# A selective state-space layer: eight passes run as one sequence of 128 states

## The reference

```
x = silu(conv(x) + conv_b);  x_dbl = x @ Wx.T      # dt (64), B (16), C (16)
dt = softplus(dt @ Wdt.T + bdt);  A = -exp(A_log)
dA = exp(dt * A);  dBx = dt * x * B                # per channel and state
h = dA_t * h + dBx_t;  y_t = sum over n of h * C_t
y = (y + x * D) * silu(z);  out = y @ W_out.T
```

## Time and profile before

| | us |
|---|---|
| median of 3 runs | 3912.1 (3908.99 to 3917.67) |
| the profiled execution | 3909.11 |
| its span, first to last instruction | 3907.3 |
| VectorE busy over the span | 2598.5 (67%) |
| PE matmul busy | 3486.0 (89%) |
| ACT busy | 2154.5 (55%) |
| POOL busy | 1405.9 (36%) |

### The profile page before, as it was taken

One profiled execution on the slowest core, in us unless ns is written; L12 is line 12 of the kernel. 1 busy time (PEld: TensorE's weight loads), 2 busy tenths in 40 slices (PEclk: granted clock), 3 DMA queues, 4 the chain that ended last, 5 costly groups with the idle time before them and its releaser, 6 DMA issues. The chain is left out here.

```text
span 3907.3 us, 135959 instructions
## 1 busy us (share of the span) xinstructions
PE 3486.0 (89%) x57850; PEld 2873.7 (74%) x57851; DVE 2598.5 (67%) x4426; ACT 2154.5 (55%) x3392; POOL 1405.9 (36%) x1363
## 2 busy tenths in 40 slices
PE   6999999999884499929999999999878888898878
PEld 4888888888674366617888888888357777788767
DVE  5777777777544122237777777776878888889964
ACT  2666666666542122205666666666467777777732
POOL 3333333333031300052333333332056666667700
PEclk8999999999896799968999999999889999999989
DMA  2001001100006110020010001000011111111100
GB/s 69 29 30 35 29 29 33 33 29 20 11 1 238 56 32 30 30 89 20 29 37 29 29 29 37 29 29 4 25 36 40 39 39 40 37 41 44 39 24 22
DMA packets 60394, 148.31 MB, mean 38 GB/s; under 512 B 8194, under 2 KB 28706, under 8 KB 59458
## 3 DMA queue, kind: packets, MB, share of 16 engines
q1 hardware_dynamic: 56770, 131.70, 10.3%
q0 software_dynamic: 3072, 8.39, 0.7%
HBM read 123.29 MB, written 16.78 MB: 36 GB/s over the span
## 5 line engine op out<-in xcount | busy, mean ns | idle before, releaser
L654 ACT ACTIVATE x_probs<-x_score_ps 128x1024 f32<-128x1024 f32 (+1 forms) x896 | 814.5, 961 | 672.5 <-PE x_score_ps L563 666.0
L714 DVE TENSOR_REDUCE x_maxes<-x_misc_ps 128x1 f32<-128x512 f32 (+1 forms) x1792 | 1022.7, 628 | 27.3 <-PE x_misc_ps L481 21.2
L1873 POOL TENSOR_TENSOR b_drive<-b_b_all,b_dtx 128x1024 f32<-128x1024 f32 x256 | 596.8, 2369 | 399.2 <-DVE b_dtx L1949 377.0
L678 POOL CAST x_kT_hi<-x_kT 128x512 fp32r<-128x512 f32 (+1 forms) x448 | 257.9, 576 | 1232.0 <-ACT x_kT L627 1116.5
L1904 DVE TENSOR_TENSOR_SCAN b_state<-b_decay_ps,b_drive 128x512 f32<-128x512 f32 x512 | 589.9, 1209 | 15.1 <-POOL b_drive L1873 12.4
L557 PE MATMUL x_score_ps<-x_qz,x_kT 32*128 32x128 f32 x13312 | 590.3, 277 | 0.3 <-DVE x_shift L724 0.2
L557 PEld LDWEIGHTS x_score_ps<-x_qz,x_kT 32*128 32x128 f32 x13312 | 501.5, 182 | 3.6 <-issue 1.5
L531 PE MATMUL x_misc_ps<-x_probs,x_v 128*32 128x64 f32 x26624 | 464.7, 221 | 0.0
L531 PEld LDWEIGHTS x_misc_ps<-x_probs,x_v 128*32 128x32 f32 x26624 | 392.4, 110 | 65.8 <-issue 23.3
L481 PE MATMUL x_misc_ps<-x_kT_hi,x_qz_hi 32*128 32x512 f32 (+1 forms) x2048 | 422.1, 406 | 6.0 <-POOL x_kT_hi L678 4.1
L1809 ACT ACTIVATE b_decay_ps<-b_dt,b_a_neg 128x504 f32<-128x504 f32 x512 | 347.9, 680 | 69.2 <-DVE b_state L1904 69.2
(11 more groups left out here) (284 smaller groups left out, 5839.4 us busy)
## 6 DMA issues: line engine op xcount, KB each, us to landing
x_raw<-in_ctxT SPq DMA_DIRECT2D x64, 800.5 KB, 4.5
b_b_all<-b_b_rows SPq DMA_DIRECT2D x128, 256.0 KB, 3.3
m_w<-in_m_w SPq DMA_DIRECT2D x16, 704.0 KB, 19.3
m_w<-in_m_w SPq DMA_DIRECT2D x8, 768.0 KB, 20.2
m_slot_rows<-m_zero SPq DMA_DIRECT2D x1, 4992.0 KB, 17.0
m_block_rows<-m_slot_rows SPq DMA_DIRECT2D x39, 128.0 KB, 2.0
m_slot_out<-m_out SPq DMA_DIRECT2D x39, 128.0 KB, 1.7
x<-in_x SPq DMA_DIRECT2D x1, 2048.0 KB, 8.3
```

What stands on the lines that cost most here:

```text
L654: nc.scalar.activation(probs[rows, s % 2, js, 0:n], score_ps[rows, js, 0:n], ACT.Exp).then_inc(exp_done, 1)
L714: nc.vector.tensor_reduce(maxes[:, c:c + m, j, k0 // NB], bank(op)[:, 0:m * even].rearrange("p (c k) -> p c k", c=m)[:, :, 0:kn], AX.X, AL ...
L1873: nc.gpsimd.tensor_tensor(drive[:, k % 2, c:c + 2, :], b_all[:, k % 2:k % 2 + 1, :].broadcast_to([P, 2, NB]), dtx[:, c:c + 2, :], ALU.mult ...
```

## The change

`recur` no longer works pass by pass. There is one loop over 128 states, and all that stood between passes is put into slots inside them.

- The raw steps of a pass, its softplus and the product `dtx` are made during the pass before. `dt` has two buffers; the steps of the first two passes are made at the start, with their softplus.
- Softplus is written another way: c = min(v, 80), and (v - c) + ln(1 + exp(c)). At the start VectorE does min, subtract and add. For passes 2 to 7 POOL does them on two chunks at a time (`cap`, `excess`, `join`). ACT does `exponential` (one in each of states 8 to 11) and `logarithm` (all four in state 12). For pass 2, whose scratch `xc` of block 0 is free only when the outputs of pass 0 are made, they stand in states 13 to 15 of pass 1.
- PE does one extra piece a state, `besides`, between two gathers: a chunk of the skip term in states 0, 13, 14, 15 (straight into the accumulator), a step chunk in states 1 to 4, an output of 128 tokens by 128 features in states 5 to 12 (in pass 1 steps 1, 2, 11, 12 and outputs 3 to 10). Steps and outputs take a turn in the two banks of `turn_ps`, by the list `USES`. ACT copies a step out (Identity with the bias), VectorE adds an output to x.
- The gates of a pass are done after the second scan of state 1 of the next pass, the products of the next pass after the second scan of state 15. The first gather of a pass (`start=True`) waits for the gates.
- `drive` is a ring of three halves instead of four. The table `wx` moves into `project`, `a_neg` takes the place of `a_log`, and the dummy activation for the table load is gone.

Core of the diff:

```diff
+    def extra(k):
+        p, n = divmod(k, NS)
+        if n == 0 or n >= NS - 3:
+            return ("skip", 0 if n == 0 else n - (NS - 4))
+        if p == 0:
+            return None
+        steps, outs = ((1, 2, 11, 12), 3) if p == 1 else ((1, 2, 3, 4), 5)
+        if n in steps:
+            return ("step", p + 1, steps.index(n)) if p + 1 < PASSES else None
+        if outs <= n < outs + 2 * TPB:
+            return ("out", p - 1) + divmod(n - outs, 2)
+        return None
+    def softplus_at(p):
+        return ((13, 14), (13, 14), (14, 14, 14, 14), 14, (15, 15)) if p == 1 else ((5, 6), (7, 8), (8, 9, 10, 11), 12, (14, 14))
+    USES = [("rows", d) for d in range(2)]
+    for k in range(STATES):
+        USES += [("tile", k, i) for i in TURNED]
+        if extra(k) is not None and extra(k)[0] != "skip":
+            USES.append(extra(k))
...
     # tensor
+        for k in range(STATES):
+            pe.wait_ge(state_done, (k + 1) * CI)
+            turn(k, 1)
+            turn(k, 0)
+            if k > 0:
+                gather(k - 1, 2)
+            if k > 0 and k % NS == 0:
+                add_total(k // NS - 1)
+            turn(k, 3)
+            turn(k, 2)
+            gather(k, 0)
+            besides(k)
+            gather(k, 1)
     # scalar
+        for k in range(STATES):
+            if k > 0:
+                read_tile(k - 1, 0)
+            make_decay(k, 2)
+            if k > 0:
+                read_tile(k - 1, 1)
+            make_decay(k, 3)
+            if k > 0:
+                read_tile(k - 1, 2)
+            if k + 1 < STATES:
+                make_decay(k + 1, 0)
+            besides(k)            # step copy of k-1; Exp, or four Ln, of pass p+1
+            if k + 1 < STATES:
+                make_decay(k + 1, 1)
     # gpsimd
+            if h >= 3:
+                pool.wait_ge(state_done, (h - 2) * 2)
+            nc.gpsimd.tensor_tensor(drive[:, h % 3, :, :], ...)
+            for half in range(2):
+                make_drive(k, half)
+            if p > 0 and p + 1 < PASSES:
+                caps, excesses, _, _, joins = softplus_at(p)
+                for half in range(2):
+                    if caps[half] == n:
+                        cap(p + 1, half)
+                    if excesses[half] == n:
+                        excess(p + 1, half)
+                    if joins[half] == n:
+                        join(p + 1, half)
     # vector
+            scan(k, 0)
+            if k > 0:
+                sum_tile(k - 1)
+            scan(k, 1)
+            if n == 1 and p > 0:
+                gate(p - 1)
+            if n == NS - 1 and p + 1 < PASSES:
+                make_dtx(p + 1)
+            scan(k, 2)
+            scan(k, 3)
+            if k > 0 and extra(k - 1) is not None and extra(k - 1)[0] == "out":
+                add_output(extra(k - 1))
```

More of the change, by code:

```diff
@@ new lines, in recur @@
+    READS = {"act": 0, "dve": 0}
+    READ_AT = {}
+    for use in USES:
+        by = "dve" if use[0] == "out" or use[0] == "tile" and use[2] == SUMMED else "act"
+        READS[by] += 1
+        READ_AT[use] = (by, READS[by])
+    SUMS = []
+    for k in range(STATES):
+        if k > 0:
+            SUMS.append(("read", k - 1, 2))
+        if k > 0 and k % NS == 0:
+            SUMS.append(("total", k // NS - 1))
+        SUMS += [("read", k, 0), ("read", k, 1)]
+    SUMS += [("read", STATES - 1, 2), ("total", PASSES - 1)]
@@ new lines, in besides @@
+        def besides(k):
+            use = extra(k)
+            p = k // NS
+            if use is None:
+                return
+            if use[0] == "skip":
+                c = use[1]
+                nc.tensor.matmul(acc_ps[:, c, :], diag[:, direction(p)[0], c, :], xc[:, direction(p)[0], c, tokens(p)],
+                                 start=False, stop=True, skip_group_check=True)
+            elif use[0] == "step":
+                step(use[1], use[2], open_bank(use)).then_inc(turn_done, 1)
+            else:
+                output(use)
@@ L1801, in _, with make_decay @@
+        gather(STATES - 1, 2)
+        add_total(PASSES - 1)
+        for i in range(TPB):
+            for h in range(2):
+                output(("out", PASSES - 1, i, h))
     @block.scalar
     def _(act):
-        def make_decay(p, n, c):
-            q = (p * NS + n) * CI + c
+        def make_decay(k, c):
+            p, n = divmod(k, NS)
+            q = k * CI + c
             if n == 0:
                 act.wait_ge(dt_done, p * CI + c + 1)
+            if n == 0 and direction(p)[1] == 0 and c < 2:
+                act.wait_ge(edge_done, direction(p)[0] * 2 + c + 1)
@@ L1817, in read_tile @@
             if k > 0:
[L1818 to L1827 removed]
+                act.wait_ge(acc_done, SUM_AT["read", k - 1, r])
@@ new lines, in besides @@
+        def besides(k):
+            use = extra(k - 1) if k > 0 else None
+            if use is not None and use[0] == "step":
+                made(act, use)
+                keep_step(use[1], use[2], bank(use)).then_inc(act_free, 1)
+            p, n = divmod(k, NS)
+            if p > 0 and p + 1 < PASSES:
+                _, _, exps, logs, _ = softplus_at(p)
+                for c in range(CI):
+                    if exps[c] == n:
+                        exponential(p + 1, c)
+                if logs == n:
+                    for c in range(CI):
+                        logarithm(p + 1, c)
@@ L1967, in feed_forward @@
+        sum_tile(STATES - 1)
+        gate(PASSES - 1)
+        for i in range(TPB):
+            for h in range(2):
+                add_output(("out", PASSES - 1, i, h))
 def feed_forward(nc, x_sb, ident, a):
```

388 lines of the change are left out of this document (194 added, 194 removed).

## The result

| us | before | after |
|---|---|---|
| median of the runs | 3912.8 (3906.3 to 3917.7, 6 runs) | 3939.9 (3931.3 to 3947.7, 6 runs) |
| profiled execution | 3909.1 | 3941.8 |
| start of the recurrence to its first scan | 21.2 | 32.7 |
| first scan to the end of the last | 825.9 | 835.4 |
| last scan to the end of the last output addition | 17.0 | 19.5 |

The ratio of after to before is 1.0071, 95% interval 1.0054 to 1.0088: 0.7% slower, where 1.3% faster was forecast. The time lies outside the range. The forecast for first to last scan was 763.5 (755.1 and the 8.4 for the lock); the trace has 835.4.

What follows compares the result with a forecast made beforehand. VectorE was taken to bound a state, and a serial chain each boundary. The states' saving of 70.8 us, less 11.5 for start and end and 8.4 for the lock, left 50.9 off 3909.1: 3858.2, as median 3861; range 3828 to 3898.

Steps and rivals of the forecast that it cites:

- State 0: First state of each steady pass: 5.15 us, the time VectorE needs for a plain state.
- Rival C: PE's clock falls in the Ln wait and at the products, 2.5 us each fall: 3891; 24% together with Rival B.
- State 1: State with the gates: 5.15 plus 2.4 plus 0.3 for the total's gather, 7.85 us.
- The minimum at 1.1: POOL's min in states 5 to 8 takes 1.1 us, a stall of 0.6 (3.2 if it costs 2.37).
- The lock: At seven boundaries, a product beside a POOL drive is held 0 to 2.37 us; middle 1.2 taken, 8.4 in all.
- Rival B: POOL sets softplus passes: min 2.37 or more, boundary products held twice by a drive: 3899; 24% together with Rival C.
- The logarithms' wait: Behind state 12's third scan: ACT's four Ln with two table loads, 4.75 us, make VectorE wait 3.5.
- The output states: States 6 to 13, bound by PE: 5.5 us each, 5.45 in pass 7.
- the step states: States 2 to 5, bound by PE: 5.34 us and 0.1, 21.5 for the four.
- rival D: The two banks do not close; output and step states go from 5.5 to 6.3 us: 3925; 10%.
- The joins: State 14: both POOL adds (4.64 us) come before state 15's drives, a stall of 1.5.
- The end of pass 1: States 13 to 15 hold all the softplus; last scan ends at 26.7 us against 20.5 plain, 6.2 more.

Runs made afterwards that it cites:

- e5: Changed kernel with four more 512-column matmul chunks per pass (passes 0 to 6), run while TensorE would idle for the products: 3925.7 us, ratio 1.0030.
- e10: e9 with the skip term's four chunks moved, two ahead of the wait for state 15, two ahead of that for state 13: 3882.2 us, ratio 0.9919.
- e9: e6 with e7's softplus states and, at the start, each chunk's exponential right behind the next chunk's copy: 3891.7 us, ratio 0.9945.
- e6: Changed kernel with e2's hold, e1's order and the gates put before state 1's second scan: 3897.0 us, ratio 0.9958.
- e3: Changed kernel without POOL's minimum, subtraction and addition in the softplus for passes 2 to 7: 3900.8 us, ratio 0.9967.
- e7: e2 with the softplus chunks of later passes spread over states 4 to 14: 3899.6 us, ratio 0.9962.
- e2: Changed kernel with POOL's first drive of a pass waiting for all four products instead of two: 3918.1 us, ratio 1.0003.
- e12: e10 with the two skip chunks ahead of state 13 moved between the turns of state 12, during the logarithms: 3863.9 us, ratio 0.9874.
- e1: Changed kernel with PE's last gather and total of the previous pass put ahead of its wait for the new pass's first state: 3938.3 us, ratio 1.0063.
- e4: Changed kernel with ACT's logarithm replaced by Exp for passes 2 to 7, so no table switch: 3919.9 us, ratio 1.0019.

## Why the prediction was wrong

Per steady pass the forecast was short by 11.1 us (10.1 to 11.1 in passes 2 to 6); passes 0, 1 and 7 were 2.4, 10.4 and 5.3 too short, which makes 71.9 over all; the start and the end add 2.6. By its own steps:

- **State 0, 5.15: the step that failed most, +4.4.** The prediction counted no work for it, though it had put the skip, the last gather and the total there on TensorE, behind turns that start late because of the products. It also dismissed the clock with "in a pass of before nothing but the boundary brought it down": the products and the gates are the boundary, moved inside, and they let TensorE idle 4.4 and 2.7 us. e5 gives the clock's share, 1.65 to 2.2 a pass; e10, against e9, gives that of the skip's chunks (6.8 or 8.1 to 5.9). Rival C had this mechanism, at the products as in the Ln wait, and 2.5 for each fall was near the price at the products.
- **State 1, 7.85: +1.5.** TensorE waits for the gates, and the sum for TensorE. That chain was in the trace of before only at the boundary and was not carried over. e6 takes it away, 7.5 us.
- **The minimum at 1.1: mis-sized, it took 2.76.** The row chosen, a cast of 0.62, was the nearest by the number of inputs; the true value lay outside both ends of the range. Of the 4.1 us of waits in states 6 to 8, 0.6 were forecast, and the rival's 3.2 was for 2.37. The prediction's own terms (3.5 short, 2.7 ahead) give 0.8 rather than 0.6. The row gives the size of the minimum; e3 and e7 show that POOL sets these states: without its softplus, or with it spread, they take 5.3 to 5.6.
- **The lock, 1.2 as a middle of 0 and 2.37: it cost 2.15 and more.** The products took 4.62 in place of 2.47 at six of the seven places, and 5.84 at the end of pass 1; e2 gives 21.8 us for it together with the clock that it brings down. The Trainium skill ("SBUF — State Buffer", SBUF: two separate sides) told this: the two lock each other out for whole instructions. The trace agrees: a product's longest is 2834 ns against a median of 683, and a drive takes 2.36. A middle between two ends was no estimate where one mechanism says which end. Rival B added that hold to POOL's shortage and came to 3899; with C's clock on top the sum passes the kernel before.
- **The logarithms' wait, 3.5: right (3.48).** The table load follows the work before it directly here too, 1.28 + 2.19 + 1.28 within 4.80. Behind it the lower clock made state 13 1.2 longer (10.2 in after, 9.0 in e12). But that cost nothing in after: the additions on POOL would have filled the time, as the 9.0 and 7.0 of e1 show, and for states 13 and 14 together the forecast of 15.8 met 16.0.
- **The output states, 5.45 to 5.5: 5.3; the step states, 21.5 for four: 5.67 each.** TensorE does bind by a few tenths: in a step state of 5.70 us (3451.2 to 3456.9) its matmuls are busy for all of it. The hand-over of the two banks held; rival D's price (3925) was the nearest to the result, but the states that it put at 6.3 take 5.3 and 5.7 wherever POOL does not hold them.
- **The joins (POOL's last additions), 1.5 in state 14: 0.5 in after**, as the long state 13 hides them; e1 and e4 bring 1.2 of them out.
- **The end of pass 1, counted to 24.6 us for states 13 to 15, or 25.8 with the 1.2 for the lock: 31.2.** It holds two minima, two subtractions and two additions of POOL; e3, without them, has 26.8.
- **Pass 0 (+2.4), the start (+1.4) and the end (+1.2)** came near. At the start POOL's first drive took 5657 ns, since VectorE's additions for pass 1 ran beside it.

So no single term explains the miss. VectorE's work was counted well, but each of the four waits was sized alone; three of them let TensorE idle, and it then does the following states at the lower clock with no slack to catch up. With the waits placed apart and TensorE filled (e12) the same work takes 97.5 us a pass. That this is close to the 98.2 of the forecast is in part luck, as its states are others (6.3 in states 9 and 11, 5.9 in state 0).

## What to carry to other kernels

Work moved off a serial boundary into a steady loop can bring the boundary's idle gaps with it: price each moved piece on the engine that waits for it, and ask whether that engine's clock survives the wait. Give independent work of the same engine (here the skip term) to each gap, and set the extra pieces of an engine that is nearly full well apart (here, three states apart they cost nothing, two apart 0.9 us, in neighbouring states up to 1.6). Where a profile shows an instruction held for the length of another engine's, as the third product was here, starting the other one later can be faster (e2).

## What the hardware showed that I had not expected

A minimum against a constant on POOL, 128x1024 in 32 bits, takes 2762 ns (2756 to 2787, 12 of them), longer than a multiplication of two tensors of that size (2362 ns), and 2.2 times the 1.25 us that twice the cast of 128x512 would make:

```profile
L1972 POOL TENSOR_SCALAR b_xc<-b_dt x12: 2756/2762/2787, 3066.9 to 3576.8; 128x1024 f32<-128x1024 f32 x12
```

At the start, one POOL multiplication took 5657 ns in place of 2362, with VectorE's additions of two tensors in SBUF beside it. In e5, after 1.0 to 1.8 us of idling, TensorE's first eight turn loads took 0.86 us at every boundary. After 2.2 us 0.86, 1.16 and 1.57 were seen in one kernel (e2), and after 4.4 to 4.6 us 1.57 in four passes of after but 0.86 in one. So the clock's fall depends on more than the gap.
